# Self-attention scores from float32r value and rest instead of float32, with keys projected two batches ahead

## What is computed

```
q = proj(Wq, bq);  k = proj(Wk, bk);  v = proj(Wv, bv)        # (B, H, S, 16)
attn1 = einsum('bhqd,bhkd->bhqk', q, k)
attn2 = einsum('bhqd,qkd->bhqk', q, rel_k[idx])               # idx: clipped distance, 41 values
attn  = softmax((attn1 + attn2) / sqrt(16))
out   = (attn @ v + einsum('bhqk,qkd->bhqd', attn, rel_v[idx])) @ Wo.T + bo
```

## Time and profile before

| | |
|---|---|
| runs | 854.18, 854.31, 852.06 us (median 854.18) |
| profiled execution | 854.72 us, span 852.9 us, mean granted clock 0.996 |
| busy share of the span | PE 94%, PE weight loads 71%, DVE 77%, ACT 71%, POOL 50% |
| chain that ended last | PE 46%, ACT 9%, DVE 5%, issue 3%, DMA 2%, POOL 1% |
| self-attention | scores from 308.1 to 567.4 us of the span |

### The profile page before, as it was taken

How to read it: one execution, slowest core, us unless ns; L and a number is a source line. 1 busy time by engine, 2 the same in 40 slices (tenths; PEclk the granted TensorE clock), 3 DMA queues, 4 the chain that set the end, 5 groups by cost and what they waited for, 6 DMA issues and landing times.

```text
span 852.9 us, 20803 instructions
## 1 busy us (share of the span) xinstructions
PE 805.5 (94%) x6837; PEld 605.5 (71%) x6837; DVE 654.1 (77%) x2466; ACT 609.7 (71%) x1595; POOL 427.7 (50%) x459
## 2 busy tenths in 40 slices
PE   9998999999999988999999999999999999999996
PEld 8876776766667766677777767667766777677785
DVE  4987778888998766777777667673888888985667
ACT  4547887888784367877877777774899999985341
POOL 2255667666644155254552534224665666425763
PEclk9999999999999999999999999999999999999999
DMA  9401761112103368977868688756122211100001
GB/s 321 157 25 45 224 194 51 55 60 81 70 15 124 124 216 269 295 218 242 277 205 268 215 247 255 239 177 212 42 66 67 66 66 66 64 2 1 26 25 50
DMA packets 105392, 115.64 MB, mean 136 GB/s; under 512 B 28589, under 2 KB 93869, under 8 KB 105030
## 3 DMA queue, kind: packets, MB, share of 16 engines
q1 hardware_dynamic: 104724, 113.97, 41.8%
q10 hardware_dynamic: 562, 0.35, 0.1%
HBM read 48.70 MB, written 51.82 MB: 118 GB/s over the span
## 4 chain that ended last, share of the span: by engine, by line
PE 46%; ACT 9%; DVE 5%; issue 3%; DMA 2%; POOL 1%; SPq 0%; DVEq 0%; ACTq 0%; POOLq 0%
PE bank L1544 7%; PE bank L242 6%; PE bank L250 4%; PE bank L2259 4%; PE bank L1559 3%; PE bank L2245 3%; ACT bias_area L2597 2%; PE bank L2276 2%; PE bank L1528 2%; PE bank L1585 2%; PE bank L1595 2%; PE bank L2309 2%; PE bank L2353 2%; PE bank L2347 2%; ACT Sx L1750 2%
## 5 line engine op out<-in xcount | busy, mean ns | idle before, releaser
L242 PE MATMUL bank<-x_feat,w_all_mats 128*128 128x256 f32 x384 | 92.7, 386 | 1.8 <-ACT q_full L358 0.6
L2994 POOL TENSOR_TENSOR bnd<-bnd,consts 128x60 f32<-128x60 f32 x64 | 18.1, 305 | 142.0 <-DMA bnd<-band_scratch 142.0
L242 PEld LDWEIGHTS bank<-x_feat,w_all_mats 128*128 128x128 f32 x384 | 70.5, 191 | 14.3 <-ACT rw L2639 3.8
L2597 ACT ACTIVATE bias_area<-bias_area,mq_two 128x256 f32<-128x256 f32 x128 | 66.2, 529 | 0.0
L1003 DVE COPY q_heads<-bank 128x512 f32<-128x512 f32 x64 | 42.0, 684 | 24.4 <-PE bank L717 24.4
L2773 DVE COPY q_heads<-bank 128x512 f32<-128x512 f32 x64 | 41.2, 683 | 23.2 <-PE bank L2259 23.2
L896 ACT ACTIVATE Sx<-Sx,mq 128x256 f32<-128x256 f32 x128 | 54.4, 498 | 5.4 <-DVE mq L995 5.4
L1750 ACT ACTIVATE Sx<-Sx,mq 128x256 f32<-128x256 f32 x128 | 54.3, 500 | 3.4 <-DVE mq L1848 3.4
L904 ACT ACTIVATE q_heads<-bank 128x512 f32<-128x512 f32 x64 | 37.8, 590 | 26.3 <-PE bank L717 26.3
L1856 DVE COPY q_heads<-bank 128x512 f32<-128x512 f32 x64 | 42.0, 684 | 17.0 <-PE bank L1544 17.0
L896 ACT ACTIVATE Pr<-Pr,mq 128x256 f32<-128x256 f32 x128 | 54.4, 502 | 0.9 <-DVE mq L995 0.9
(11 more groups left out here) (309 smaller groups left out, 2384.8 us busy)
## 6 DMA issues: line engine op xcount, KB each, us to landing
dist<-skew_scratch SPq DMA_DIRECT2D x64, 296.0 KB, 4.1
skew_scratch<-rw SPq DMA_DIRECT2D x30, 588.0 KB, 4.5
bnd<-band_scratch SPq DMA_DIRECT2D x64, 108.0 KB, 2.6
band_scratch<-bias_area SPq DMA_DIRECT2D x32, 162.0 KB, 2.5
band_scratch<-bias_area SPq DMA_DIRECT2D x32, 148.0 KB, 2.1
skew_scratch<-dist SPq DMA_DIRECT2D x4, 1024.0 KB, 7.1
context_values<-dist SPq DMA_DIRECT2D x8, 512.0 KB, 2.6
v_two<-context_values SPq DMA_DIRECT2D x8, 512.0 KB, 4.3
```

The costliest lines, as they stand in the source:

```text
L242: last = pe.matmul(dst[:, m * S:(m + 1) * S], w[:, k, m * P:(m + 1) * P], rhs[:, k, :], start=(k == 0), stop=(k == FT - 1))
L2597: last = act.activation(rows_of(n, g)[:, t, :], rows_of(n, g)[:, t, :], ACT.Exp, bias=mq_two[:, n % 2, g, t:t + 1], scale=-1.0, accum_out= ...
```

## The change

Scores of batches 1 to 7 come from float32r parts. Weights and biases of q and k (and `rel_k`, and the columns `head*`) are laid out so that the two heads of a tile lie on even and odd rows. GpSimd makes a rounded value and the rest of q (`split_q`) and of k (new `split_k`); SyncE's queue moves rows between neighbouring partitions (new `turn_q`, `turn_k`, six transfers for a batch), so that a tile of 32 rows holds value and rest of one head. A round then has 16 products in float32r, in pairs that add up, for 8 in float32. Batch 0 stays in float32, with `pair` masks for the former `half` masks. Keys are projected two batches ahead: `project_k(1)` and `project_k(2)` lie in batch 0, `project_k(b + 2)` in batches 1 to 5, none in batch 6. `copy_k` writes to one whole-key buffer. The new cells need a tile `spare` of 14 KB in each partition; the reserve for descriptors made by software, `dynamic_dma_scratch_size`, is set to 1024 bytes.

```diff
+        spare = sb("spare", [P, 7, FT, S])
...
                     def scores(n):
                         b, j = divmod(n, NQ)
-                        if j == 0:
-                            pe.wait_ge(k_sb, b + 1)
-                        pe.wait_ge(q_split, FT * b + j % 2 + 1)
+                        if n == 0:
+                            pe.wait_ge(k_sb, 1)
                         ge(pe, s_max, TT * 4 * n)
+                        if b == 0:
+                            pe.wait_ge(q_split, j % 2 + 1)
+                        elif j == 0:
+                            pe.wait_ge(q_turned, 16 * 2 * b)
+                            pe.wait_ge(k_turned, 16 * 4 * b)
                         for t in range(TT):
-                            for g in range(4):
...
+                            for i in range(2 if b else 1):
+                                for g in range(4):
...
+                                        last = pe.matmul(s_bank[g][:, t * S:(t + 1) * S],
+                                                         q_cells[b % 2][r, j % 2, j // 2, q],
+                                                         k_cells[b % 2][i][r, j % 2, j // 2, :],
+                                                         start=(i == 0), stop=(i == 1))
...
                     def first_round(b, n):
...
                             else:
-                                pe.wait_ge(qf_sb, FF_EARLY + 2)
+                                pe.wait_ge(k_sb, 3)
                             turn_normed(b + 2)
                         if b < B:
                             turn(n, 0)
                             turn(n, 1)
                             if b == 0:
                                 pe.wait_ge(r_sb, 4 + 1)
+                                project_k(1)
+                                turn(n, 2)
+                                pe.wait_ge(k_sb, 2)
...
                             project_v(b)
                         if 1 <= b <= B:
                             turn_bands(n - 2)
-                        if b < B:
+                        if 1 <= b < B:
                             turn(n, 2)
                         if b < B - 1:
                             pe.wait_ge(v_sb, b + 1)
                             rel_scores(b + 1, 1)
                         if b < B:
                             turn(n, 3)
-                        if b < B - 1:
+                        if 1 <= b < B - 2:
                             pe.wait_ge(r_sb, 4 * (b + 1) + 2)
-                            project_k(b + 1)
+                            project_k(b + 2)
                         if 1 <= b <= B:
                             weigh(n - 1)
                         if b == 0:
-                            pe.wait_ge(k_sb, 2)
+                            pe.wait_ge(r_sb, 4 + 2)
                             turn_normed(2)
...
                     def second_round(b, n):
...
-                                pe.wait_ge(k_sb, b + 2)
+                                pe.wait_ge(k_sb, b + 3)
                             ternary_product(b + FF_EARLY)
...
                     def fourth_round(b, n):
...
+                        if b == 0:
+                            pe.wait_ge(qf_sb, FF_EARLY + 2)
+                            project_k(2)
...
                     def copy_k(b):
                         dve.wait_ge(k_mm, b + 1)
-                        ge(dve, s_mm, NQ * (b - 1))
+                        ge(dve, k_low_made, b - 1)
                         for m in range(FT):
-                            last = dve.tensor_scalar(k_two[:, b % 2, m, :], m_bank[:, m * S:(m + 1) * S],
-                                                     kb[:, m:m + 1], None, ALU.add)
+                            last = dve.tensor_scalar(k_whole[:, m, :] if b else spare[:, 0, m, :],
+                                                     m_bank[:, m * S:(m + 1) * S], kb[:, m:m + 1], None, ALU.add)
...
+                            if j == 0 and b < 2:
+                                copy_k(b + 1)
...
-                            if j == 1 and b < B - 1:
-                                copy_k(b + 1)
+                            if j == 1 and 1 <= b < B - 2:
+                                copy_k(b + 2)
...
                     def split_q(b):
                         pool.wait_ge(q_sb, b + 1)
+                        if b == 0:
...
+                            return
                         ge(pool, s_mm, NQ * (b - 1))
-                        for e in range(2):
-                            pool.tensor_scalar(q_par[:, b % 2, e, :, :], q_full[:, :, :], col(f"half{e}"), None,
-                                               ALU.mult).then_inc(q_split, 1)
+                        pool.tensor_copy(q_cells[b % 2][:, :, :, :],
+                                         q_full[:, :, :].unsqueeze(1).broadcast_to([P, 2, FT, S])).then_inc(q_split, 1)
+                        pool.wait_ge(q_split, FT * b + 1)
+                        ge(pool, q_turned, 16 * 2 * (b - 1))
+                        pool.tensor_tensor(q_low[:, :, :], q_full[:, :, :], q_cells[b % 2][:, 0, :, :], ALU.subtract)\
+                            .then_inc(q_split, 1)
+
+                    def split_k(b):
+                        value, rest = k_cells[b % 2]
+                        pool.wait_ge(k_sb, b + 1)
+                        ge(pool, s_mm, NQ * (b - 1))
+                        k = k_whole.unsqueeze(1).broadcast_to([P, 2, FT, S])
+                        pool.tensor_copy(value[:, :, :, :], k).then_inc(k_high_made, 1)
+                        pool.wait_ge(k_high_made, b)
+                        pool.tensor_tensor(rest[:, :, :, :], k, value[:, :, :, :], ALU.subtract).then_inc(k_low_made, 1)
...
+                            if j == 1 and b == 0:
+                                split_k(1)
+                            if j == 0 and 2 <= b < B - 1:
+                                split_k(b + 1)
                             if 1 <= n <= NQ * B:
                                 mask_bands(n - 1)
+                            if j == 0 and b == 1:
+                                split_k(2)
...
+                    def turn_q(b):
+                        sp.wait_ge(q_split, FT * (b + 1))
+                        q, low = q_cells[b % 2][:, :, :, :].bitcast(F32), q_low[:, :, :].bitcast(F32)
+                        sp.dma_start(q[1:P:2, 0, :, :], low[0:P:2, :, :]).then_inc(q_turned, 16)
+                        sp.dma_start(q[0:P:2, 1, :, :], low[1:P:2, :, :]).then_inc(q_turned, 16)
+
+                    def turn_k(b):
+                        sp.wait_ge(k_low_made, b)
+                        value, rest = (c[:, :, :, :].bitcast(F32) for c in k_cells[b % 2])
+                        sp.dma_start(value[1:P:2, 0, :, :], rest[0:P:2, 0, :, :]).then_inc(k_turned, 16)
...
                             if n >= 2 and n + 2 < NQ * B:
                                 load_dist(n + 2)
+                            if j == 0 and b < B - 1:
+                                turn_q(b + 1)
+                            if j == 1 and b < B - 1:
+                                turn_k(b + 1)
```

43 lines of the change are left out of this document (31 added, 12 removed).

## The result

The changed kernel takes 863.61 us (median of six runs, 858.45 to 869.94) against 854.18 us (six runs, 852.06 to 854.35): 1.0116 times as long, 95% interval 1.0074 to 1.0158. That is slower by 9 to 10 us, where I had said 854.0 and at most 859. The profiled execution is the shortest of the six, 858.45 us with a span of 856.6 us and a mean granted clock of 0.997; the others have 0.986 to 0.997.

What follows compares the result with a forecast made beforehand. PE looked like the bound, but waits for ACT in fourth rounds and DVE in first rounds. Gains 5.9 and losses 5.8 us net -0.1 against the profiled 854.72; on the 854.18 median, 854.0 us, range 847 to 859.

Steps and rivals of the forecast that it cites:

- The pitch: Time on PE from one score block's start to its successor's: 0.67 us in the new form instead of 1.08.
- the worth of the products: Faster score blocks gain 0.41 us each in 11 second and third rounds, 4.5 us, plus 0.2 in batch 7.
- the chain in batch 0: First round of batch 0: projecting k(1) before the values delays ACT's copy of relative scores and the whole batch by 3.7 us.
- k(2): End of batch 0: its projection adds 1.9 us to PE and a copy, of which about 0.6 us is left.
- the copy of k(3): Batch 1: DVE's copy waits for GpSimd's split of k(2), two us late; loss 0.8 us, range 0.4 to 1.5.
- batch 6: The keys' projection there goes, 1.9 us less to the next start; ACT's late exponentials leave a gain of 1.2 us.
- Rival A: PE is the bound throughout and all 28 score blocks count, 11.5 us gained: 847.3 us; chance 0.12.
- the two points without slack: PE waits for ACT's relative-score copy in fourth rounds and DVE's value copy in first rounds; faster blocks there gain nothing.
- Rival B: Batch 0 takes up its own delay, so 3.7 + 0.6 us of loss fall away: about 850 us; chance 0.18.
- GpSimd otherwise: Batches 2 to 6: the keys' split, 3.4 us, fits GpSimd's 7.78 us idle time before the bands and costs nothing.
- SP's queue and the DMA engines: Six added issues and transfers per batch mostly fit waits and idle time: loss 0.5 us, bounds 0 to 6.
- rival C: Turned rows collide with skewed-row loads at batch starts, about 1 us more at each of six boundaries: 859.5 us; chance 0.18.

Runs made afterwards that it cites:

- the last version: Changed kernel with splits and turns moved, batch 0 in its former order, and third fill and its store earlier: 851.20 us against 854.76, ratio 0.9951.

## Why the prediction was wrong

**What was right.** The pitch (0.68 for 0.67), the worth of the products (2.6 to 4.7 us for 4.5 to 4.7; 0.40 us in ten of the 11 second and third rounds that I had counted, nothing in the second round of batch 6), the chain in batch 0 (4.1 us for 3.7, ACT's copy 0.4 us later than I put it), k(2) and the copy of k(3) that waits for the split (together +1.3 for 1.4; PE waits 1.34 us there), and batch 6, which falls short in the changed kernel (0.95 less for 2.0) and comes to 1.7 in the last version. Rival A was wrong for the reason I gave: PE is not the bound at the two points without slack. Rival B was right in part: of the 4.1 us in batch 0, 2 to 3 remain in the time.

**The first step that failed** is "GpSimd otherwise": "In batches 2 to 6 `split_k` falls into an idle time of 7.78 us before the bands, which covers its 3.4: nothing." The cover was real, and I asked only who waits for GpSimd. I had found that DVE's chain at the boundary has no slack, and did not ask what GpSimd's work does to DVE while it runs. It costs 4.3 us in the kernel before (1.0052), and none of it in the third round (1.0004): not a mis-sized term but a missing one. At its boundaries all of it is PE's wait for the values behind DVE's lengthened copy (3.6 us of 3.8 in the first rounds). The rows show what it does: a DVE operation from SBUF to SBUF ends 0.28 us after the GpSimd instruction that it meets. The Trainium skill states this rule in SBUF — State Buffer, section SBUF: two separate sides: DVE in a two-port mode and GpSimd arbitrate for a shared pair of ports, by "an exclusive lock, not a bandwidth split". By that rule the copy of the inverses had to be priced at up to 2.4 us instead of 0.43, as often as it meets a subtraction. The traces agree with it in each case above. For the split of the queries I had compared only its length with that of the mask products ("no longer than the present one"). It is shorter, but DVE's clip, rounding and subtraction, which the mask products had held up to 2.25 us, take up to 3.05 beside it, and PE waits 0.49 us for that in batch 3: a smaller part of the same step.

**The second** is the sum's 0.5 us for "SP's queue and the DMA engines". The transfers cost 4.1 us in the kernel before by the ratio, and 2.1 in the changed one, where the intervals overlap. That lies within my bounds of 0 to 6, and rival C had 6; but neither the step nor the rival had the place. I had written of the delayed issues that "behind them are only stores and loads that are needed a round or two later", and of the fill only in batch 1, at 0.2 us. I did not follow the one whose landing ACT awaits before it may reuse the rows: bands, mask, normalisation, fill, store, copy of relative scores, in the fourth round, which I had myself named as a point without slack. With the fill and the store earlier, the transfers are free by the ratio (1.0001).

**How the sum comes out.** In the profiled execution: batch 0, k(2) and k(3) 5.4 us for 5.1; the rest of the stage -0.1 for -5.1. The 5 us between lie where the two steps above act: the first rounds of batches 2 to 6 are 3.3 us longer in all than forecast, and the fourth rounds of batches 1 to 3 are 2.5 us longer; the other rounds give a little back. That gives +3.7 us in the span, as the stage also began 1.6 us earlier. The median is 5 us above this execution. One profile of such a time shows the same waits longer; why the landings vary so much more from one execution to the next than before is left open. The clock is not the main cause: with it held through batch 0 the median is 863.81 us.

## What to carry to other kernels

Idle time of an engine is no proof that work put there is free: look at what the neighbours do in that time, and at GpSimd work beside DVE's copies from SBUF to SBUF first of all, where the same 3.4 us cost 4 us or nothing. When transfers are added, follow each wait for a landed store, not only the loads: the buffer that is reused after a store is on the path when its user has no slack. And where a change is a sum of gains and moves, time the moves alone; here a change that made the kernel 1.2% slower became one of 0.5% faster with the same products.

## What I had not expected of the hardware

- Beside a GpSimd cast or subtraction of 1024 elements a partition (1.04 and 2.4 us), DVE's copy of 128x512 float32 from SBUF to SBUF took up to 2.46 us instead of 0.43, and one of its tensor-scalar operations 2.50 instead of 0.43 to 0.79; each ended 0.28 us after the GpSimd instruction. Reciprocals, sums from a bank and the statistics were not slowed.
- Gaps of 1.66, 0.78 and 3.15 us on PE within 10 us let the granted clock fall from 2.4 to 1.2 GHz for some microseconds in six of seven profiled executions; 25 small products in these gaps kept it up.
- Six transfers of 128 KB per batch on engines that are about 80% busy over a batch made the mask of a band in batch 1 start 62.9 us after the first scores instead of 57.7, where PE was 1.6 us late; with transfers 32 times smaller, which SP issues just as often, it started at 59.2.
